# Transposes of the middle tiles: from TensorE to VectorE squares and a trip through DRAM

## Time and profile before

| | |
|---|---|
| median of 3 runs | 1982.6 us |
| lowest, highest | 1982.26, 1984.07 us |
| profiled execution, first to last instruction (its span) | 1981.5 us |
| mean granted TensorE clock | 0.996 |
| PE matmul busy | 1961.9 us, 99% |
| DVE, ACT, POOL busy | 1289.0 (65%), 1020.0 (51%), 406.8 us (21%) |
| DMA | mean 23 GB/s, nearly all of it at the start |

### The profile page before, as it was taken

The page is one execution under the profiler, slowest core; times in us unless marked ns, Lnnn a source line. Parts: engine busy times, 40 slices in busy tenths (PEclk is TensorE's granted clock), DMA queues, the critical chain, the costliest instruction groups (busy, mean ns, idle before and its releaser), DMA issues.

```text
span 1981.5 us, 37810 instructions
## 1 busy us (share of the span) xinstructions
PE 1961.9 (99%) x15288; PEld 1895.6 (96%) x15288; DVE 1289.0 (65%) x3292; ACT 1020.0 (51%) x1786; POOL 406.8 (21%) x344
## 2 busy tenths in 40 slices
...
GB/s 359 224 3 1 22 1 12 11 2 22 1 22 1 1 22 1 22 1 1 22 1 22 1 1 22 1 22 1 23 1 1 22 1 12 1 1 12 1 1 23
DMA packets 24538, 46.03 MB, mean 23 GB/s; under 512 B 1264, under 2 KB 21488, under 8 KB 24176
## 3 DMA queue, kind: packets, MB, share of 16 engines
...
...
## 4 chain that ended last, share of the span: by engine, by line
PE 97%; DMA 1%; DVE 1%; SPq 1%; issue 0%; ACT 0%; POOL 0%; DVEq 0%; ACTq 0%
PE ffn_fill L1117 49%; PE att_fill L1048 25%; PE ffn_fill L1048 13%; PE ffn_fill L1174 6%; PE att_fill L1136 1%; PE att_fill L1252 1%; DMA scratch_w2T<-in_w2T 1%; DMA w<-scratch_w1T 0%; SPq L543 0%; PE ffn_fill L1285 0%; DVE late_sm L869 0%; PE ffn_fill L1280 0%; ACT late_kv_b L1009 0%; DVE st L671 0%; DVE late_prob_t_lo L864 0%
## 5 line engine op out<-in xcount | busy, mean ns | idle before, releaser
L1117 PE MATMUL ffn_fill<-act_hi,h 128*128 128x256 f32 x4096 | 987.2, 283 | 0.8 <-issue 0.2
L1117 PE MATMUL ffn_fill<-act_lo,h 128*128 128x256 f32 x4096 | 978.2, 280 | 1.2 <-issue 1.2
L1117 PEld LDWEIGHTS ffn_fill<-act_hi,h 128*128 128x128 f32 x4096 | 770.3, 188 | 9.2 <-POOL act_lo L649 3.9
L1117 PEld LDWEIGHTS ffn_fill<-act_lo,h 128*128 128x128 f32 x4096 | 773.1, 189 | 3.6
L976 ACT ACTIVATE whole<-ffn_fill,scales 128x256 f32<-128x256 f32 x512 | 214.0, 469 | 291.3 <-PE ffn_fill L1117 290.1
L649 POOL TENSOR_TENSOR act_lo<-whole,act_hi 128x512 fp32r<-128x512 f32 x128 | 166.8, 1303 | 492.4 <-DVE act_hi L798 492.4
L802 DVE TENSOR_TENSOR act_lo<-whole,act_hi 128x512 fp32r<-128x512 f32 x256 | 183.4, 716 | 112.0 <-ACT act_hi L980 109.7
L1048 PE MATMUL ffn_fill<-half_hi,w 128*128 128x256 f32 x1024 | 245.9, 283 | 0.0
L1048 PE MATMUL ffn_fill<-half_lo,w 128*128 128x256 f32 x1024 | 244.3, 281 | 0.0
L1048 PEld LDWEIGHTS ffn_fill<-half_lo,w 128*128 128x128 f32 x1024 | 193.3, 189 | 0.1
L1048 PEld LDWEIGHTS ffn_fill<-half_hi,w 128*128 128x128 f32 x1024 | 192.5, 188 | 0.4 <-issue 0.2
...
## 6 DMA issues: line engine op xcount, KB each, us to landing
x<-in_L_attn_x SPq DMA_DIRECT2D x16, 512.0 KB, 3.3
out<-x SPq DMA_DIRECT2D x15, 512.0 KB, 2.9
...
```

The lines of the kernel that those rows point to most:

```text
L1117: last = pe.matmul(two(bank)[:, o, :], view(w), view(moving[:, k, :]), start=k == 0 and o == 0 and half == 0, stop=k == KH - 1 and half == ...
```

## The change

- LT is gone from BODY; both places now use T. DVE transposes 32 by 32 squares in place of position with one instruction (into in_blocks), SP writes the tile to DRAM (spread), waits, and reads it back in four DMAs of 32 partitions each, in pieces of 32 floats, so that the squares come to their places (placed). ACT makes the high part, POOL (not DVE) the low part.
- a:T and NT go the same way, each one DVE instruction in place of 16.
- CP is gone from BODY. CX takes its place: DVE transposes squares of kv_b into xn (CXa), SP does the round trip back into kv_b, ACT copies the high part once CO of the number before has filled its bank, DVE subtracts (CXb). The exp of CS2 and CS3 waits for the low part of CX0 and CX1.
- The orders of BODY are new on every engine, and SP has an order of its own. FIRST changes in n:NT0 alone, END not at all.

```
@@ -95,6 +95,7 @@
     "CZ": {"att_fill": 2, "z_hi_ready": 2},
     "CS": {"att_fill": 1, "row_max": 2, "exp_bias": 1},
     "CP": {"att_fill": 1, "prob_hi_ready": 1},
+    "CX": {"prob_turned": 1, "p_spread": 16, "p_placed0": 64, "p_placed1": 64, "prob_hi_ready": 1, "prob_lo_ready": 1},
     "CO": {"att_fill": 1, "inverse": 1},
     "CF": {"att_fill": 2, "tanh_done": 2, "out_ready": 1},
...
@@ -148,8 +151,8 @@
 
 
 PLAN = steps_from("""
-    U0 c:CST U1 U2 U3 c:CNO G0 c:LT c:CB c:CQ G1 c:CV c:CZ G2 c:CS0 G3 c:CP0 c:CS1 c:CS2 c:CO0 c:CP1 c:CS3
-    H0 c:CO1 c:CP2 H1 c:CO2 BST1 c:CP3 BNO1 a:AST H2 c:CO3 c:DST H3 NT1 NTL1 c:DNO W0 c:LT a:ANO U0 U1 c:CF a:T
+    U0 c:CST U1 U2 U3 c:CNO G0 c:T c:CB c:CQ G1 c:CV c:CZ G2 c:CS0 c:CS1 c:CS2 c:CS3 G3 c:CX0
+    c:CO0 c:CX1 H0 c:CO1 H1 BST1 BNO1 a:AST H2 c:CX2 c:CO2 c:CX3 c:CO3 c:DST H3 NT1 NTL1 c:DNO W0 c:T a:ANO U0 U1 c:CF a:T
     U2 U3 a:AB a:AKV0 a:AKV1 a:AKV2 G0 a:AKV3 G1 G2 a:AS a:AQ a:AM G3 a:AO H0 H1 n:BST0 n:BNO0 H2 H3 n:NT0 n:NTL0
...
@@ -247,9 +250,9 @@
     m:BT0 a:AKV2 a:AKV3 U0 U1 a:AS a:AQ U2 CHECK1 U3a a:AM U3b G0a a:AO G0b G1 G2 G3a FOLD0 CHECK2 G3b H0a
     CHECK3 H0b H1 H2 H3 BT1 W0 U0 U1 U2 U3 G0 G1 G2 G3 H0 H1 H2 H3 W1"""),
     "BODY": order_from("""
-    U0 U1 U2 U3 G0 G1a c:LT G1b c:CV c:CZ G2a c:CS0 G2b G3a c:CP0 c:CS1 c:CS2 G3b c:CO0 c:CP1 c:CS3 H0a
-    c:CO1 c:CP2 H0b c:CO2 c:CP3 H1 c:CO3 H2 H3 W0 U0 c:LT U1 U2 U3 c:CFa G0a c:CFb G0b G1 G2 G3 a:AKV0
-    a:AKV1 a:AKV2 a:AKV3 H0a a:AS a:AQ a:AM H0b H1a a:AO H1b H2 H3 W1"""),
+    U0 U1 U2 U3 G0 G1 G2 c:CV c:CZ c:CS0 c:CS1 G3a c:CS2 c:CS3 G3b H0 H1a c:CO0 c:CO1 H1b H2 H3a
+    c:CO2 c:CO3 H3b W0 U0 U1 U2 U3 G0 G1a c:CF G1b G2 G3a a:AKV0
+    a:AKV1 a:AKV2 a:AKV3 G3b a:AS a:AQ a:AM H0 a:AO H1 H2 H3 W1"""),
     "END": order_from("""
     U0 U1 U2 U3 G0 G1 G2 G3 H0 H1 H2 H3 BT1 W0 U0 U1 U2 U3 G0 G1 G2 G3 H0 H1 H2a c:LT H2b H3 W1 c:CV c:CZ
...
     n:NTL0 G3 H0 H1 H2 H3 W1"""),
     "BODY": order_from("""
-    c:CSTa U0 U1 U2 U3 c:CSTb c:CNO c:LT c:CQ c:CV c:CZ c:CS0 G0 c:CP0 c:CS1 c:CS2 c:CO0 G1 c:CP1 c:CS3 G2
-    G3 c:CO1 c:CP2 c:CO2 BST1 c:CP3 H0 BNO1 a:AST c:CO3 c:DSTa H1 c:DSTb NT1a H2 NT1b H3 NTL1 c:DNO W0 U0 U1
-    c:LT U2 U3 a:ANO c:CF a:Ta a:Tb G0 G1 a:AKV0 a:AKV1 G2 a:AKV2 a:AKV3 a:AS G3 a:AQ a:AM a:AO n:BST0 H0
-    n:BNO0 H1 n:NT0a H2 n:NT0b H3 n:NTL0 W1"""),
+    c:CSTa U0 c:CSTb U1 U2 c:CNO c:T U3 G0 c:CQ G1 G2 c:CV c:CZ c:CS0 c:CS1 c:CX0a c:CX1a BST1 c:CS2 c:CS3 BNO1
+    NT1 G3 a:AST H0 c:CX0b c:CX1b c:CX2a c:CX3a c:CO0 c:CO1 H1 NTL1 H2 c:CX2b c:CX3b c:CO2 c:CO3 c:DST H3 c:DNO c:T W0 U0 U1
+    a:ANO U2 a:T U3 G0 G1 c:CF G2 a:AKV0 a:AKV1 a:AKV2 a:AKV3 G3 a:AS a:AQ a:AM H0 a:AO n:BST0 H1
+    n:BNO0 n:NT0 H2 H3 n:NTL0 W1"""),
     "END": order_from("""
...
     "BODY": order_from("""
-    U0 U1 U2 U3 c:LT G0 G1 c:CV c:CZ c:CS0 c:CP0 G2 c:CS1 c:CS2 c:CP1 G3 c:CS3 c:CP2 H0 c:CP3 H1 H2 H3 NT1
-    U0 U1 c:LT U2 U3 c:CF G0 a:T G1 G2 a:AKV0 a:AKV1 a:AKV2 a:AKV3 G3 a:AQ a:AM H0 H1 H2 H3 n:NT0"""),
+    U0 U1 U2 U3 G0 G1 c:T G2 c:CV c:CZ c:CS0 c:CS1 G3 H0 c:CX0 c:CS2 c:CX1 c:CS3 H1 NT1 H2 c:CX2 c:CX3 H3
+    U0 U1 U2 U3 G0 c:T G1 c:CF a:T G2 a:AKV0 a:AKV1 a:AKV2 a:AKV3 G3 a:AQ a:AM H0 H1 H2 H3 n:NT0"""),
     "END": order_from("""
     U0 U1 U2 U3 G0 G1 G2 G3 H0 H1 H2 H3 BT1 U0 U1 U2 U3 G0 G1 G2 G3 H0 H1 c:LT H2 H3 c:CV c:CZ d:LT c:CS0
     c:CS1 c:CP0 d:CV d:CZ c:CP1 d:CS0 c:CS2 c:CS3 c:CP2 d:CS1 d:CP0 c:CP3 d:CS2 d:CP1 d:ET0 d:CS3 d:CP2
     d:EF0 d:ET1 c:LT d:CP3 d:EF1 c:CF d:ET2 d:EF2 d:ET3 d:EF3"""),
 }
+SP_ORDERS = {
+    "FIRST": order_from("FOLD0 n:NT0"),
+    "BODY": order_from("c:T c:CX0 c:CX1 NT1 c:CX2 c:CX3 c:T a:T c:CF n:NT0 W1"),
+    "END": order_from("c:CF d:EF0 d:EF1 d:EF2 d:EF3"),
+}
 POOL_ORDERS = {
     "FIRST": order_from("""
     p:AST a:AST p:AB m:BST0 U0 U1 U2 U3 a:AB BST1 U0 U1 U2 U3 n:BST0"""),
...
@@ -576,28 +590,54 @@
             sp.wait_ge(w_bounced[3][0], 16)
             land(3, "w3T", w3[:])
 
-            c = Counts(phases[0])
-            for step in FIRST:
-                if step[:2] == ("FOLD", 0):
+            def turn_blocks(c, made, free, whole, scratch, into, spread, placed):
+
+                nb = into.shape[1]
+                sp.wait_ge(s[made], c.value(made, 1))
+                wait(sp, s[placed], c.value(placed))
+                wait(sp, s[free], c.value(free))
+                sp.dma_start(scratch, whole[:]).then_inc(s[spread], 16)
+                sp.wait_ge(s[spread], c.value(spread, 16))
+                spots = scratch.rearrange("(q i) (m c j) -> c i m q j", i=SQ, c=P // SQ, j=SQ)
+                for there in range(P // SQ):
+                    rows_there = into[there * SQ:(there + 1) * SQ].rearrange("p b k (q j) -> p (b k) q j", j=SQ)
+                    sp.dma_start(rows_there, spots[there]).then_inc(s[placed], 16)
+
+            def part(step, c, slots):
+                kind, j, who = step
+                if kind == "FOLD":
                     wait_taken(sp, c, "att_fill", 0)
                     wait_taken(sp, c, "att_fill", 1)
-                c.ahead(step)
-            for t in range(2, SLOTS):
-                sp.dma_start(x[:, t], x_in[t]).then_inc(x_loaded[t], 16)
-
-            for t in range(T - SLOTS):
-                sp.wait_ge(s["out_ready"], t + 1)
-                sp.dma_start(x_out[t], x[:, t % SLOTS]).then_inc(x_stored, 16)
-                sp.wait_ge(x_stored, 16 * t + 16)
-                sp.dma_start(x[:, t % SLOTS], x_in[t + SLOTS]).then_inc(x_loaded[t % SLOTS], 16)
-            for t in range(T - SLOTS, T):
-                if t == T - 1:
-                    for b in range(NB):
-                        sp.wait_ge(s["late_out_ready"], b + 1)
-                        sp.dma_start(x_out[t][:, b], x[:, t % SLOTS, b]).then_inc(x_stored, 16)
-                else:
+                    for t in range(2, SLOTS):
+                        sp.dma_start(x[:, t], x_in[t]).then_inc(x_loaded[t], 16)
+                elif kind == "T":
+                    turn_blocks(c, "turned", "xt_lo_ready", in_blocks, a["scratch_turn"], turned, "spread", "placed")
+                elif kind == "CX":
+                    r, scratch, placed = j % 2, a["scratch_prob"][j % 2], f"p_placed{j % 2}"
+                    sp.wait_ge(s["prob_turned"], c.value("prob_turned", 1))
...
+                    sp.wait_ge(s["late_out_ready"], j + 1)
+                    sp.dma_start(x_out[T - 1][:, j], x[:, (T - 1) % SLOTS, j]).then_inc(x_stored, 16)
+
+            walk(part, SP_ORDERS)
             sp.wait_ge(x_stored, 16 * (T - 1 + NB))
 
...
@@ -651,8 +691,8 @@
                 elif kind == "T":
                     for k in range(KD):
                         wait_apart(pool, s[own.own + "xt_hi_ready"], c.value(own.own + "xt_hi_ready", k + 1))
-                        pool.tensor_tensor(own.xt[1][:, k, :], turned[:, k, :], own.xt[0][:, k, :].bitcast(F32),
-                                           ALU.subtract).then_inc(s["xt_lo_ready"], 1)
+                        pool.tensor_tensor(by_token_block(own.xt[1][:, k, :]), turned[:, :, k, :],
+                                           by_token_block(own.xt[0][:, k, :].bitcast(F32)), ALU.subtract).then_inc(s["xt_lo_ready"], 1)
                 elif kind == "CF":
                     for g in range(2):
...
@@ -757,33 +797,20 @@
                     norm = "ANO" if who in "ap" else "DNO" if ("DNO", 0, who == "d") in c.seen else "CNO"
                     dve.wait_ge(s[own.own + "xn_ready"],
                                 c.value(own.own + "xn_ready", c.ago(own.own + "xn_ready", norm, 0, who == "d") + NB))
-                    wait(dve, s["xt_lo_ready"], c.value("xt_lo_ready"))
-                    for there in range(P // 2 if share == "b" else 0, P // 2 if share == "a" else P, SQ):
-                        for here in range(0, P, SQ):
-                            into = turned[there:there + SQ].rearrange("p k (b n) -> p b k n", b=NB)
-                            last = dve.transpose(into[:, :, :, here:here + SQ],
-                                                 own.xn[here:here + SQ].rearrange("p b (k n) -> p b k n", k=KD)
-                                                 [:, :, :, there:there + SQ])
-                    if share != "a":
-                        last.then_inc(s["turned"], 1)
+                    wait(dve, s["spread"], c.value("spread"))
+                    dve.transpose(in_blocks[:], own.xn[:].rearrange("p b d -> p (b d)")).then_inc(s["turned"], 1)
                 elif kind == "BT":
                     bank, out = filled(dve, c, "ffn_fill", 0)
                     dve.wait_ge(s["bt_hi"], c.value("bt_hi", 1))
                     dve.tensor_tensor(half_lo[:], two(bank), half_hi[:].bitcast(F32), ALU.subtract).then_inc(out, 1)
...
@@ -863,6 +890,15 @@
                     dve.wait_ge(s[own.own + "prob_hi_ready"], c.value(own.own + "prob_hi_ready", 1))
                     dve.tensor_tensor(own.prob_t[1][:], four(bank), own.prob_t[0][:].bitcast(F32), ALU.subtract)\
```

(31 more changed lines are left out.)

51 lines of the change are left out of this document (34 added, 17 removed).

## The result

The changed kernel takes 2412.1 us (median of 4 runs, 2404.3 to 2414.9) against 1983.3 in the same comparison: ratio 1.2155, 95% interval 1.2134 to 1.2175. It is slower by 429 us. The profiled run took 2404.3 and has a span of 2402.6, 421 more than before's. The forecast was 2258, with 2160 to 2420 as the range for 8 in 10.

What follows compares the result with a forecast made beforehand. PE bounds the kernel: 22.2 us of stands per body, less 3.5 of removed transposes and 0.1 of present standing, times 14 is +260; with +15 for the clock the span is 2256, the median 2258. Range for 8 in 10: 2160 to 2420.

Steps and rivals of the forecast that it cites:

- dearer DMA piece: Gather pieces through DRAM at 48 ns in place of 16: +27 us a body, 2640; at 30 ns about +10, 2400.
- Twelve items: PE's stands walked one by one through a body's new orders, 22.2 us per body in sum.
- (a): First-half G0 waits for U3, behind DVE's statistics, CNO and T and POOL's low part: PE stands 2.4 us a body.
- (f): CO1 waits for CX1, whose copy follows CS2's exp and a table load on ACT: PE stands 2.2 us.
- (h): CO3 directly after CO2; CX3's copy waits until CO2's bank is full: PE stands 1.5 us, DMA just in time.
- (k): AKV0 waits for a:T: PE stands 3.1 to 4.4 us, taken as 3.9; the upper value if tanh loads a table.
- I take 0.7 of a fall per body, +15: PE's clock falls to half after stands of 4 us: none to two a body, 0 to +42 us, taken as +15.
- (j): CF waits for c:T, which ACT does after G0 and its gelu table load: PE stands 4.1 us.
- all is hidden: Rival: everything added is hidden and PE's 3.5 us a body are gained, 1934 us; 8% for faster by any amount.
- the gather is the bound: Rival: the DMA gather through DRAM, pieces at 30 ns or more, is the bound: 2400 to 2640 us; chance 15%.
- SP's queue: Rival: SP's queue serialises, CO2's and CO3's stands grow 2 to 4 us each: 2300 to 2370; 15 of the likeliest's 66 in 100.
- (b): CV waits for the first c:T, squares in place at 18.8, low part at 22.3: PE stands 1.0 us.

Runs made afterwards that it cites:

- the fourth run: The changed kernel with VectorE's U3 put ahead of c:CNO and the first c:T in BODY: 2448.8 us, ratio 1.2342.

## Why the prediction was right, and what it mis-sized

**The sign and the place.** Stands of PE where two instructions are neighbours in the lists, and not the DMA, make the kernel slower. That part was right. The time is in the range for 8 in 10 by only 8 us, and it is over the 2190 to 2370 that the prediction gave this very mechanism; the end at 2420 was drawn with a dearer DMA piece in mind, which did not come. So that the range held is in part luck. Twelve items were forecast at 22.2 us a body; they are 23.0, with errors of both signs that nearly cancel:

| | a | b | c | d | e | f | g | h | i | j | k | l |
|---|---|---|---|---|---|---|---|---|---|---|---|---|
| forecast | 2.4 | 1.0 | 1.75 | 0.8 | 1.2 | 2.2 | 1.1 | 1.5 | 2.0 | 4.1 | 3.9 | 0.2 |
| measured | 3.4 | 1.0 | 1.7 | 0.8 | 1.3 | 1.6 | 1.1 | 2.2 | 2.1 | 4.1 | 3.5 | 0.3 |

Three are off by more than 0.5. (a): CNO took 2.35 us, not the 1.38 of the earlier trace rows, and a cast 0.84, not 0.43. (f): from the end of CX0's low part (1100.75) to CO1's first matmul (1104.22) 3.5 us pass, near the 3.6 of the sum; but PE starts CO0 only 0.26 after that end and is shown busy with it for 1.65, not 1.4. (h): the DMA is in it; without the trip it is 1.50, the value forecast. (k) came without the table load that the walk left open.

**The clock, the term that failed.** The step "I take 0.7 of a fall per body, +15" was far too small. The profiled span went up by 421:

| us over the run | forecast | measured |
|---|---|---|
| stands in the bodies | 311 | 327.5 |
| PE's transposes and the stands of before gone | -51 | -51 |
| clock | 15 | 113 |
| the rest: PE's first and last matmul at a stand | 0 | 32 |

The 113 is the count over the whole span. I had seen the fall in the earlier trace rows and named (j) and (k) as places for it; the count and the length failed: about three falls a body and not 0.7, (a) among them, and 5.5 to 6 us of work at half speed behind (j) and (k) where I had put 3. The end of my own range, two falls, would have been 42. The runs agree on the mechanism: the granted clock rose when the stands were filled (0.943 to 0.984), when one was taken away (0.959) and when the orders left none over 2.2 us (0.991). The run with the filled stands is the direct test, as nothing else was changed in it.

**The refill**, the rest of the table, wasn't in the sum. In the rows below the slot of the first matmul after a stand is 0.23 us and not 0.117, and the last one before it counts its full 0.27. The run is the one with the new orders:

```profile
1118.36 0.27 PE L1156 MATMUL ffn_fill<-act_lo,h 128*128 128x256 f32 x1
1119.17 0.39 PE L1156 MATMUL ffn_fill<-act_hi,h 128*128 128x256 f32 x1 [0.54 <-POOL act_lo L683]
1119.40 0.28 PE L1156 MATMUL ffn_fill<-act_lo,h 128*128 128x256 f32 x1
```

Together that is 0.27 us beside this stand. It is not that much at each: 12 stands in 14 bodies would make 45 us, where 32 are to be explained, about 0.2 a stand. A body of that run shows that the term is there without the clock: at 1.00 PE is busy 120.12 us, 3.0 more than 120.62 - 3.5. No run was made to isolate it.

**The trip's price.** 13.4 ns a piece against 16; but from the end of DVE's transpose to ScalarE's start on the squares 9.75 us (the fourth run) against 2.9 + 5.8 = 8.7. I gave no price to SP's issue, and it has one: 2.75 us for four gather DMAs. The Trainium skill ("VectorE: DVE Perf Modes", section "The three transpose paths") says that a plain copy with strides is 19 times slower than the DMA's own transpose when the innermost stride of the destination is large. The prediction left that condition out. Here the innermost 32 floats stay together on both sides, so the rule does not speak of this pattern, and no run here tests it; 128 KB land in 3.7 us, and the gather's 55.8 us of the 16 engines are about twice the 25.6 of the plain load in the earlier trace rows.

**The rivals.** That all is hidden (1934) fails in the given orders and in the ones laid anew, where 7.4 us of stands a body stay. That the gather is the bound gives a time near the measured one (2400 to 2640) and is still wrong: 18 us of 429 go with all the DMAs. A time in a rival's range was no evidence for it here. SP's queue does serialise, but PE pays at most the 0.7 of (h) for it, 12.5 us over the run (88.7 for prob_t_lo, 76.2 without the trip). CX3's squares are transposed at 1105.81, and SP, busy with CX2's trip, issues their spread 4.3 us later; ScalarE's copy then waits for the DMA:

```profile
1110.08 0.57 SPq L619 DMA_DIRECT2D scratch_prob<-xn  x1
```

```profile
1117.09 0.63 ACT L1057 ACTIVATE prob_t_hi<-kv_b 128x512 fp32r<-128x512 f32 x1 [3.37 <-DMA kv_b<-scratch_prob]
```

**What (b) hid.** The walk made each stand alone, with PE's arrival taken from the stands before it. It didn't ask what comes last if one of them goes. The prediction had the squares of the first c:T in place at 18.8 and ScalarE there at 19.0, a lead of 0.2 us for the trip; when PE came earlier, the trip decided, and the fourth run found it. Of the 104 us that the refitted orders still lose, I have no run that divides them between the trips' length and the orders.
